# Graph layer in split float32 on one core: the first chunk's work reordered between the engines

## The reference, cut to what matters

```
h   = maximum((x - mean) / sqrt(var + 1e-5), 0)     # x: 4096 x 128, adj: 4096 x 4096
out1 = conv(h,  adj, eps1, W1, b1);  out2 = conv(x2, adj, eps2, W2, b2)
out  = x + concat(out1, out2, axis=1) @ Wm.T + bm
# conv: ax = a @ x; h = ax + (1 + eps) * ax; three times h = relu(h @ W[i].T + b[i])
```

## Time and profile before

| | |
|---|---|
| median of 3 runs | 415.06 us (414.89 to 415.4) |
| the profiled execution, its own time | 414.96 us |
| its span in the trace | 413.1 us |
| PE busy | 404.5 us, 98% of the span |
| DVE, ACT, POOL busy | 220.4, 218.9, 34.1 us |

### The profile page before, as it was taken

One profiled execution on the slowest core, in us unless ns is written; L12 is line 12 of the kernel. 1 busy time (PEld: TensorE's weight loads), 2 busy tenths in 40 slices (PEclk: granted clock), 3 DMA queues, 4 the chain that ended last, 5 costly groups with the idle time before them and its releaser, 6 DMA issues.

```text
span 413.1 us, 4963 instructions
## 1 busy us (share of the span) xinstructions
PE 404.5 (98%) x1747; PEld 326.8 (79%) x1747; DVE 220.4 (53%) x274; ACT 218.9 (53%) x271; POOL 34.1 (8%) x37
## 2 busy tenths in 40 slices
PE   7999989999999999999999999999999999999996
PEld 2887768888888888888888888888888888888884
DVE  5899975452834456434555426455273454755222
ACT  5888892355543354553435554335554335765032
POOL 1443460000100000000100001000010000000100
PEclk9899999999999999999999999999999999999999
DMA  7998568432755508355293444843265541740100
GB/s 254 396 411 314 203 225 309 188 122 98 254 203 203 195 33 287 144 203 203 80 332 109 152 191 149 308 160 130 116 236 221 203 176 52 267 167 1 52 0 25
DMA packets 14745, 76.15 MB, mean 184 GB/s; under 512 B 2000, under 2 KB 2256, under 8 KB 6928
## 3 DMA queue, kind: packets, MB, share of 16 engines
q1 hardware_dynamic: 13392, 71.97, 46.8%
q0 software_dynamic: 1200, 3.93, 2.8%
q10 hardware_dynamic: 144, 0.13, 0.1%
HBM read 73.93 MB, written 2.10 MB: 184 GB/s over the span
## 4 chain that ended last, share of the span: by engine, by line
PE 85%; DVE 6%; ACT 5%; issue 2%; DMA 1%; SPq 1%; ACTq 0%; DVEq 0%
PE acc L429 25%; PE acc L433 25%; PE acc L430 25%; DVE adj_lo L386 3%; PE hidden L430 3%; PE hidden L429 3%; PE hidden L433 2%; ACT adj_hi L257 2%; DMA adj_raw<-adj_tiles 1%; DVE stats L354 1%; PE merged L430 1%; PE merged L429 1%; PE merged L433 1%; ACT x_rows L274 1%; DVE var_eps L359 1%
## 5 line engine op out<-in xcount | busy, mean ns | idle before, releaser
L429 PE MATMUL acc<-adj_hi,feat_lo 128*128 128x512 f32 x448 | 175.0, 391 | 1.6 <-ACT act_f L241 1.6
L433 PE MATMUL acc<-adj_lo,feat_hi 128*128 128x512 f32 x448 | 174.8, 390 | 0.0
L430 PE MATMUL acc<-adj_hi,feat_hi 128*128 128x512 f32 x448 | 174.3, 389 | 0.0
L330 DVE TENSOR_TENSOR adj_lo<-adj_raw,adj_hi 128x2048 fp32r<-128x2048 f32 x56 | 128.2, 2327 | 26.7 <-ACT adj_hi L224 26.7
L336 DVE TENSOR_TENSOR act_lo<-act_f,act_hi 128x512 fp32r<-128x512 f32 x60 | 41.4, 691 | 124.7 <-ACT act_f L241 124.7
L224 ACT ACTIVATE adj_hi<-adj_raw 128x2048 fp32r<-128x2048 f32 x56 | 104.8, 1930 | 2.2 <-PE acc L433 2.0
L429 PEld LDWEIGHTS acc<-adj_hi,feat_lo 128*128 128x128 f32 x448 | 84.1, 188 | 19.6 <-issue 2.0
L240 ACT ACTIVATE act_hi<-hidden,bias 128x512 fp32r<-128x512 f32 x45 | 31.0, 688 | 129.1 <-PE hidden L433 129.1
L433 PEld LDWEIGHTS acc<-adj_lo,feat_hi 128*128 128x128 f32 x448 | 84.1, 188 | 18.2
L430 PEld LDWEIGHTS acc<-adj_hi,feat_hi 128*128 128x128 f32 x448 | 84.1, 188 | 18.0
L240 ACT ACTIVATE act_hi<-acc,ax_scale 128x512 fp32r<-128x512 f32 x15 | 10.3, 688 | 44.7 <-PE acc L433 44.7
(11 more groups left out here) (60 smaller groups left out, 200.5 us busy)
## 6 DMA issues: line engine op xcount, KB each, us to landing
adj_raw<-adj_tiles SPq DMA_DIRECT2D x61, 1024.0 KB, 5.1
x_rows<-x_tiles SPq DMA_DIRECT2D x16, 256.0 KB, 6.4
adj_raw<-adj_tiles SPq DMA_DIRECT2D x12, 256.0 KB, 6.2
x_res<-x_t POOLq DMA_DIRECT2D x8, 256.0 KB, 6.2
out_t<-y_sb POOLq DMA_DIRECT2D x7, 256.0 KB, 2.3
w_raw<-w_t SPq DMA_DIRECT2D x1, 512.0 KB, 9.0
out_t<-y_sb SPq DMA_DIRECT2D x1, 128.0 KB, 1.8
out_t<-y_sb ACTq DMA_DIRECT2D x1, 128.0 KB, 1.9
```

The costliest lines, as they stand in the source:

```text
L330: nc.vector.tensor_tensor(adj_lo[:, u % RING, :], adj_raw[:, u % RING, :], f32(adj_hi[:, u % RING, :]), ALU.subtract).then_inc(lo_made, 1)
L429: nc.tensor.matmul(out, lhs_lo, rhs_hi, start=start, stop=False)
L430: nc.tensor.matmul(out, lhs_hi, rhs_hi, start=False, stop=False)
L433: return nc.tensor.matmul(out, lhs_hi, rhs_lo, start=False, stop=stop)
```

## The change

All of it is in chunk 0 and its seam to chunk 1.

- SP: `x2` is loaded ahead of `x`; a block of units 1 and 2 is issued only when the same block of the unit before has landed; `x` of a unit comes behind its blocks; the weights come with unit 3.
- POOL: it rounds `x2` of units 1 to 7 and blocks 1 and 2 of unit 1 (both `tensor_copy`, listed as CAST); the low part of `x` is made two units behind; the weights' two parts leave it.
- ACT: it rounds only `x2` of unit 0; `rectify` and the rounding of `x` run one unit behind, and the root stands behind them; it rounds the weights behind the root of unit 5.
- DVE: `variances` stands between the second and third block of its unit, `scale_and_shift` behind the fourth; it makes the low part of the weights after unit 7.
- PE: branch 0 of unit u runs behind branch 1 of unit u + 1; its low features come last; two products on zeros (`FILLERS`) stand behind each of the first four; `WARM_UP` is 11.
- ACT and DVE read out branch 1's accumulator after unit 0 of each next chunk, branch 0's after unit 1.

```diff
-    WARM_UP = 12
+    POOL_BLOCKS = (1, 2)
+    WARM_UP = 11
+    FILLERS = 2
+    WEIGHTS_AT = U - 3
...
-    OPERAND_AFTER = {1: 0, 3: 1, 5: 2, 7: 3}
+    OPERAND_AFTER = {0: ((0, BRANCH_ORDER[0]),), 1: ((0, BRANCH_ORDER[1]),),
+                     **{u: tuple((k, b) for b in BRANCH_ORDER) for u, k in {3: 1, 5: 2, 7: 3}.items()}}
...
+            load_x2(0)
+            load_x(0)
+            for j in range(JB):
+                load_block(0, j)
+            for u in range(1, FINE_LOADS):
+                for j in range(JB):
+
+                    if j < FINE_SIGNALS:
+                        sp.wait_ge(fine_loaded[(u - 1) * FINE_SIGNALS + j], 16)
+                    else:
+                        sp.wait_ge(raw_loaded[u - 1], 16)
+                    if j == 0:
+                        load_x2(u)
+                    load_block(u, j)
+                load_x(u)
+            for u in range(FINE_LOADS, U):
+                load_x2(u)
+                load_unit(0, u)
+                load_x(u)
+                if u == WEIGHTS_AT - 2:
...
+            def high_of_x2(u):
+                pool.wait_ge(x2_loaded[u % X_SLOTS], 16 * (u // X_SLOTS + 1))
+                nc.gpsimd.tensor_copy(feat_hi[:, 1, u * JB:(u + 1) * JB, :], x2_rows[:, u % X_SLOTS]).then_inc(
+                    feat2_hi_made, 1)
...
+            low_of_x2(0)
+            high_of_x2(1)
+            low_of_x2(1)
+            for j in POOL_BLOCKS:
+                cols = slice(j * CW, (j + 1) * CW)
+                pool.wait_ge(fine_loaded[FINE_SIGNALS + j], 16)
+                nc.gpsimd.tensor_copy(adj_hi[:, 1, cols], adj_raw[:, 1, cols]).then_inc(pool_hi_made, 1)
+            for u in range(2, U):
+                high_of_x2(u)
+                low_of_x(u - 2)
+                low_of_x2(u)
+            low_of_x(U - 2)
+            low_of_x(U - 1)
...
-            for u in range(U):
-                high_of_x2(u)
+            high_of_first_x2()
+            fine_high(0, 0)
+            fine_high(0, 1)
+            std_of_x(0)
+            fine_high(0, 2)
+            fine_high(0, 3)
+            fine_high(1, 0)
+            rectify(0)
+            fine_high(1, JB - 1)
+            high_of_x(0)
+            std_of_x(1)
+            for u in range(2, U):
+                fine_high(u, 0)
+                fine_high(u, 1)
+                fine_high(u, 2)
+                fine_high(u, 3)
+                rectify(u - 1)
+                high_of_x(u - 1)
                 std_of_x(u)
-                for j in range(JB):
-                    fine_high(u, j)
-                rectify(u)
+                if u == WEIGHTS_AT:
+                    act.wait_ge(w_loaded, 16)
+                    nc.scalar.activation(w_hi[:, :, :], w_raw[:, :, :], ACT.Copy).then_inc(w_hi_made, 1)
+            rectify(U - 1)
+            high_of_x(U - 1)
...
-            for u in range(U):
+            variances(0)
+            fine_low(0, 0)
+            scale_and_shift(0)
+            for j in range(1, JB):
+                fine_low(0, j)
+            for j in range(JB):
+                fine_low(1, j)
+            variances(1)
+            scale_and_shift(1)
+            for u in range(2, U):
+                fine_low(u, 0)
+                fine_low(u, 1)
                 variances(u)
+                fine_low(u, 2)
+                fine_low(u, 3)
                 scale_and_shift(u)
-                for j in range(JB):
-                    fine_low(u, j)
+            dve.wait_ge(w_hi_made, 1)
+            nc.vector.tensor_tensor(w_lo[:, :, :], w_raw[:, :, :], f32(w_hi[:, :, :]),
+                                    ALU.subtract).then_inc(w_lo_made, 1)
...
             for u in range(U):
-                for b in BRANCH_ORDER:
-                    first_aggregate(u, b)
+                first_aggregate(u, first)
+                if u > 0:
+                    first_aggregate(u - 1, late)
+            first_aggregate(U - 1, late)
```

More of the change, by code:

```diff
@@ L402, in _ @@
                     low_of_unit(c, u)
-                    if u in OPERAND_AFTER:
-                        low_of_operand(c - 1, OPERAND_AFTER[u])
+                    for k, b in OPERAND_AFTER.get(u, ()):
+                        low_of_branch(c - 1, k, b)
                 result(c - 1)
@@ L433, in product, with idle_products, low_features, low_block @@
                 return nc.tensor.matmul(out, lhs_hi, rhs_lo, start=False, stop=stop)
+            def idle_products(n):
+                for _ in range(n):
+                    nc.tensor.matmul(merged[:, :], zeros[:, 0:P], zeros[:, :], start=True, stop=True)
             def columns(u, j):
                 return u % RING, slice(j * CW, (j + 1) * CW)
+            def low_features(u, b):
+                pe.wait_ge(feat2_lo_made if b else feat1_lo_made, u + 1)
+                for j in range(JB):
+                    s, cols = columns(u, j)
+                    last = nc.tensor.matmul(acc[b][:, :], feat_lo[:, b, u * JB + j, :], adj_hi[:, s, cols],
+                                            start=False, stop=(b != FIRST_BRANCH and u == U - 1 and j == JB - 1))
+                return last
+            def low_block(u, b, j):
+                s, cols = columns(u, j)
+                return nc.tensor.matmul(acc[b][:, :], feat_hi[:, b, u * JB + j, :], adj_lo[:, s, cols], start=False,
+                                        stop=(b == FIRST_BRANCH and u == U - 1 and j == JB - 1))
             def first_aggregate(u, b):
                 fine = b == FIRST_BRANCH
-                pe.wait_ge(feat2_hi_made if b else feat1_hi_made, u + 1)
+                if not b:
+                    pe.wait_ge(feat1_hi_made, u + 1)
+                elif u == 0:
+                    pe.wait_ge(first_feat2_hi_made, 1)
+                else:
+                    pe.wait_ge(feat2_hi_made, u)
                 if not fine:
@@ L454, in first_aggregate @@
                                      start=(u == 0 and j == 0), stop=False)
[L456 to L470 removed]
+                    if fine and u == 0:
+                        idle_products(FILLERS)
+                if fine:
+                    low_features(u, b)
+                    for j in range(JB):
+                        if j < FINE_SIGNALS:
+                            pe.wait_ge(fine_lo_made, u * FINE_SIGNALS + j + 1)
+                        else:
+                            pe.wait_ge(lo_made, u + 1)
+                        last = low_block(u, b, j)
+                else:
+                    pe.wait_ge(lo_made, u + 1)
+                    for j in range(JB):
+                        low_block(u, b, j)
+                    last = low_features(u, b)
                 signal(u, b, last)
@@ L536, in _ @@
             pe.wait_ge(zeros_made, 1)
-            for _ in range(WARM_UP):
-                nc.tensor.matmul(merged[:, :], zeros[:, 0:P], zeros[:, :], start=True, stop=True)
+            idle_products(WARM_UP)
             for u in range(U):
-                for b in BRANCH_ORDER:
-                    first_aggregate(u, b)
+                first_aggregate(u, first)
+                if u > 0:
+                    first_aggregate(u - 1, late)
+            first_aggregate(U - 1, late)
             with pe.Fori(1, LAST) as c:
```

92 lines of the change are left out of this document (36 added, 56 removed).

## The result

The changed kernel takes **423.74 us** (median of 4 runs, 423.3 to 424.65) against 415.23 us for the kernel before in the same comparison (414.89 to 415.47): ratio 1.0203, 95% interval 1.019 to 1.0216, so 8.5 us slower. The forecast was 423.5. The profiled execution has an own time of 424.65 and a span of 422.7 us, 9.6 more than before's 413.1; it is the slowest of the four, so its differences are about 1 us above those of the medians.

What follows compares the result with a forecast made beforehand. PE was taken as the bound nearly everywhere, with DVE and POOL excluding each other in chunk 0's 5.92 us turn. The walk gave +9.3, of which +8.5 was taken: 415.0 + 8.5 = 423.5 us, range 415 to 427.5.

Steps and rivals of the forecast that it cites:

- (c): Steady units of chunk 0: POOL's three operations meet DVE's subtractions, DVE waits 2.4 us, turn 7.2 instead of 5.92.
- The rule weighed: Whether POOL's rounding, reading one tensor, also shuts DVE out: bounds 0 and 0.5 us per rounding, 0.5 taken.
- The rival in which the roundings pass: POOL's roundings run beside DVE: start 3 us earlier, turn 6.9, +5.7, 420.7 us; chance 0.2.
- (a): ACT loses the rounding of `x2`, 0.54 us a unit, 3.8 over seven units; worth nothing on the path.
- (b): POOL gets more work: a 128x512 rounding taken as 0.6 us, 3.1 us per unit in all.
- (d): Start of chunk 0: ACT begins unit 2 at 18.3, units 3 to 7 at 22.7, 29.3, 36.5, 43.7, 50.9.
- (e): Chunk 0's end: late branch a unit behind lengthens it; PE starts chunk 1 at 66.3, third product waits until 67.4.
- (f): Start of chunk 1: PE's wait of 1.6 us, counted within the sum; read-out no longer behind two roundings.
- (g): Start of chunk 0: fillers may save 2.4 us at most, counted 0; one warm-up product less 0; held loads 0.
- Faster: Chunk 0: POOL blocks DVE under 0.6 us a unit, PE is the bound again, 411 us; chance 0.16.
- The clock falls too: Chunk 0: PE's waits bring two or three half-clock stretches, 1.5 us each, 427 us; chance 0.07.
- It does nothing: Chunk 0: turn stays near 5.9, ACT's gain is idle anyway and POOL hides, 415 us; chance 0.05.

Runs made afterwards that it cites:

- run 1: The changed kernel with POOL's sixteen subtractions of chunk 0 replaced by zero fills of the same size: 414.25 us.
- run 6: The kernel before, each unit's first rounding and subtraction put ahead of root and small operations, low part of `x2` moved from POOL to DVE: 412.11 us.
- 11: The changed kernel with the low part of `x2` of units 1 to 7 moved from POOL to DVE: 419.9 us.
- run 2: The changed kernel with POOL's roundings (`x2` of units 1 to 7, blocks 1 and 2 of unit 1) given back to ACT: 422.97 us.
- run 4: The kernel before with only the change's accumulator read-out, branch 1 after unit 0 and branch 0 after unit 1 of each next chunk: 414.34 us.
- run 7: The kernel of run 6 with the accumulator read-out of run 4 added: 412.16 us.
- run 8: The kernel before with only the change's two fillers behind each of the first four products and 11 warm-up products: 415.35 us.
- 12: The kernel before with only the change's waits that hold a block's load until the same block of the unit before has landed: 415.8 us.
- run 3: The changed kernel without the waits that hold a block's load until an older block has landed: 425.11 us.
- run 10: The kernel before with only PE's late branch one unit behind and its low features last: 416.04 us.
- 9: The kernel of run 7 with the change's fillers and 11 warm-up products added: 412.1 us.

## Why the prediction was right, step by step

**What bounds the kernel, and (c) the collision**: right, and shown by runs 1, 6 and 11 from three sides. Run 1 alone would leave the rival that POOL is merely slow; that DVE's own operations are long only while POOL's read, and that the time falls when a subtraction is moved to the busier DVE, excludes it. Its size was right (2.4 us a unit; a turn of 7.11 for 7.2), its place off by one operation: POOL's first subtraction meets `var_eps` and not the third subtraction. The prediction said "as ACT's root becomes due"; ACT's rounding in fact ends 1.43 before the root, since ACT is ready early and waits. The three pieces were taken as 1.0, 1.15 and 0.3 and measured 1.1, 1.08 and 0.2 (run 2 gives 0.2 for the last). One sentence was wrong: that DVE's operations with one tensor input run beside POOL. `var_eps` has one and was held for 1.1; the prediction had read the same, smaller, at its 0.41. And of the signs that it named, ACT's idle time before `rectify` came to 1.07, not to 2; the rest stands before the root.

**The rule weighed**: the rounding on POOL, which reads one tensor, is held by DVE (1.07 instead of 0.62) and holds DVE (`newton` ends with it). Earlier, in unit 3, it meets a pair of subtractions, which takes 1.71 instead of 1.29:

```profile
27.19 1.71 DVE L447 TENSOR_TENSOR adj_lo<-adj_raw,adj_hi 128x512 fp32r<-128x512 f32 x2
27.22 1.13 POOL L228 CAST feat_hi<-x_rows 128x512 fp32r<-128x512 f32 x1 [0.57 <-DMA x_rows<-x_tiles]
```

The Trainium skill ("SBUF — State Buffer", section "Who interferes with whom") lets a DVE instruction with two SBUF inputs contend with a GpSimd instruction that reads SBUF, and the trace agrees. The rival in which the roundings pass is refuted; its 420.7 was 3 us from the result, and even run 2, with no rounding on POOL at all, takes 422.97. So a rounding's hold of 0.5 was too large in both: it is 0.2 in a steady turn, and all four together move the start by 0.4.

**(a) Less for ACT is worth nothing**: right. ACT idles 1.43 + 1.07 in a turn.

**(b) POOL's rounding**: taken as 0.6, measured 0.62 where nothing holds it.

**(d) The start** was too short. Forecast for units 2 to 7: 18.3, 22.7, 29.3, 36.5, 43.7, 50.9. Trace: 19.1, 23.5, 31.2, 38.3, 46.3, 52.5 (at unit 6 the rounding of the weights, 1.04, stands ahead of it). Of the 1.6 us at the end, 0.8 is there at unit 2, where the first block landed 0.6 later than in the trace of before and ACT waited 4.5 us in all for blocks (no term of the sum for that); 1.1 comes in the turn from unit 3 to unit 4, 7.7 instead of 6.6; and 0.3 goes again in the later turns, 7.1 instead of 7.2. Later landing is not the change's doing for certain: over the profiles of these kernels ACT's first rounding, which waits for that block, begins anywhere between 5.9 and 7.9 us, with no tie to the holds.

**(e) The tail** was 1.1 us too long: unit 7's last two subtractions meet no POOL operation and take 1.28, where 2.2 was taken, because POOL's had already fallen on `var_eps`. The late start and the short tail cancel: chunk 1 at 66.75 for 66.3, the third product at 67.94 for 67.4.

**The sum** was +9.3, the profiled execution says +9.6, and the medians +8.5. I took 0.8 off for the bound with a hold of 1.0, which the measured 1.1 and 1.08 do not bear out, and by chance the profiled execution lies 0.9 above the median. The closeness of 423.5 to 423.74 is partly luck: a start 1.6 too short and a tail 1.1 too long nearly cancel, and nothing in the runs stands behind the 0.8. Good to about 1 us is what the walk deserves.

**(f) The seam**: read as 1.6 us of wait, worth 1.2 when the rest is unchanged (run 4), nothing on top of the new order (run 7). **(g)** fillers and held loads at 0: right when each is added to the kernel before (runs 8 and 12); within the changed kernel the holding seems worth about 1 us (run 3), for which the sum had nothing.

**The rivals.** *Faster* named the point that decides, under 0.6 us of blocking in a unit. Runs 6 and 7 cross it, and the PE is the bound again, at 412.1. The changed kernel is at 2.4. *The clock falls too* came once, for 2 to 3 us, and was swallowed by a wait that would have come anyway. *It does nothing* fails on the turn, 7.11 instead of 5.92.

Shown: the collision is the loss (run 1), it is removed or halved by taking work from the engine that looks idle (runs 6, 11), and none of roundings, held loads, fillers, seam or the late branch makes it alone (runs 2, 3, 8, 4, 10, 12). Left open: what binds the first 19 us together with the roundings; why run 3 is slower; whether the fillers keep the clock; whether 9 beats 7; and moving the low part of `x2` to DVE without the new order wasn't tried, nor was a turn of 7.1 without the late branch behind.

## What to carry to other kernels

An engine at 10% busy can be the one that costs: before moving work to it, look at what its present operations do to its neighbour, in the few operations that are longer than their shape allows. Tiny operations that end at the same instant as another engine's are the mark. And a change of several parts should be timed by parts: this one held a part that gains 1.2 us when timed alone (the seam) under a loss of 8.5.

## What was not expected of the hardware

- A DVE operation on 128x4 with one tensor input (`var_eps`, 0.17 in run 1) waits as long as a large subtraction: 1.1 us, until POOL's ends. Its statistics don't: 0.86 beside POOL's subtraction in run 6, as without it.
- POOL's fill of 128x512 (0.53 us) leaves DVE's subtractions at 0.65 each. What takes DVE's turn is POOL's subtraction or rounding, not that POOL works.
- Both queues full, the two engines take turns, one operation each; a subtraction handed to POOL then costs DVE 1.1 us and would cost 0.6 on DVE itself.
- The time from which ACT can round the first block differs by up to 1.95 us between kernels whose first loads are issued the same way (5.94 in run 8, 7.89 in run 10, one trace of each).
